# First attention: block-diagonal queries with 128-row maxima and score products, and the negated maxima sent by transfer into a contraction row

## The reference

```python
def _L0_xattn_ref(q, k, v, Wq, bq, Wk, bk, Wv, bv, Wo, bo):   # 16 heads of 8
    qh = (q @ Wq.T + bq).reshape(B, S, H, Hd).transpose(0, 2, 1, 3)
    kh = (k @ Wk.T + bk).reshape(B, S, H, Hd).transpose(0, 2, 1, 3)
    vh = (v @ Wv.T + bv).reshape(B, S, H, Hd).transpose(0, 2, 1, 3)
    scores = jnp.einsum('bhqd,bhkd->bhqk', qh, kh) / jnp.sqrt(jnp.float32(Hd))
    attn = jax.nn.softmax(scores, axis=-1)
    out = jnp.einsum('bhqk,bhkd->bhqd', attn, vh)
    out = out.transpose(0, 2, 1, 3).reshape(B, S, D)
    return out @ Wo.T + bo
x = x + _L0_xattn_ref(_layernorm(x, axis=-1), ctx_1024, ctx_1024, ...)
x = x + _L0_ffn_ref(_layernorm(x, axis=-1), ...)      # then the second layer
```

## Time and profile before

| | us |
|---|---|
| median of 3 runs (1695.71 to 1699.17) | 1699.14 |
| the profiled execution | 1695.49 |
| its span, first to last instruction | 1693.7 |
| TensorE matmul busy | 1401.0 (83%) |
| VectorE busy | 949.1 (56%) |
| ScalarE busy | 814.0 (48%) |
| GpSimd busy | 661.4 (39%) |

### The profile page before, as it was taken

One profiled execution on the slowest core, in us unless ns is written; L12 is line 12 of the kernel. 1 busy time (PEld: TensorE's weight loads), 2 busy tenths in 40 slices (PEclk: granted clock), 3 DMA queues, 4 the chain that ended last, 5 costly groups with the idle time before them and its releaser, 6 DMA issues. The chain is left out here.

```text
span 1693.7 us, 31779 instructions
## 1 busy us (share of the span) xinstructions
PE 1401.0 (83%) x11720; PEld 1123.0 (66%) x11720; DVE 949.1 (56%) x2066; ACT 814.0 (48%) x1335; POOL 661.4 (39%) x556
## 2 busy tenths in 40 slices
PE   0599999806599999999993798988988989836698
PEld 0477777606488888888882477777777777736486
DVE  0455544337656665666563666665666666527665
ACT  0255655521344444444442465655656556521354
POOL 1266656602155555555552123333232332412254
PEclk9999655555799999999996899998999899965799
DMA  4211111040000000000001000000000000010000
GB/s 114 75 39 39 46 63 45 2 149 1 1 1 1 1 1 1 0 0 0 0 0 62 1 2 1 2 1 3 2 1 3 2 1 2 2 32 1 1 25 25
DMA packets 27575, 31.59 MB, mean 19 GB/s; under 512 B 4721, under 2 KB 21682, under 8 KB 27314
## 3 DMA queue, kind: packets, MB, share of 16 engines
q1 hardware_dynamic: 27442, 29.75, 5.7%
HBM read 23.45 MB, written 6.29 MB: 18 GB/s over the span
## 5 line engine op out<-in xcount | busy, mean ns | idle before, releaser
L1347 POOL TENSOR_TENSOR w_lo_f<-weighted_f,w_hi_f 128x512 fp32r<-128x512 f32 x232 | 300.6, 1296 | 345.8 <-ACT w_hi_f L1289 345.8
L565 POOL TENSOR_TENSOR p_lo_l<-probs_l,p_hi_l 128x512 f16<-128x512 f32 x128 | 148.2, 1158 | 336.5 <-ACT p_hi_l L358 336.5
L1327 DVE TENSOR_TENSOR hidden_f<-psum,gate_act_f 128x512 f32<-128x512 f32 x232 | 160.5, 692 | 210.0 <-PE psum L1239 199.3
L1304 ACT ACTIVATE gate_act_f<-psum 128x512 f32<-128x512 f32 x232 | 138.7, 598 | 269.0 <-PE psum L1239 267.6
L916 POOL TENSOR_TENSOR p_lo_a<-probs_a,p_hi_a 128x1024 f16<-128x1024 f32 x64 | 135.9, 2127 | 112.9 <-ACT p_hi_a L808 112.9
L1333 DVE TENSOR_TENSOR weighted_f<-psum,hidden_f 128x512 f32<-128x512 f32 x232 | 160.5, 692 | 9.0
L1239 PE MATMUL psum<-x_lo_f,w_hi 128*128 (+1 forms) x384 | 153.8, 401 | 0.0
L1237 PE MATMUL psum<-x_hi_f,w_hi 128*128 (+1 forms) x384 | 152.0, 396 | 1.8 <-PEq L1135 1.8
L1238 PE MATMUL psum<-x_hi_f,w_lo 128*128 (+1 forms) x384 | 151.8, 395 | 0.0
L1289 ACT ACTIVATE w_hi_f<-weighted_f 128x512 fp32r<-128x512 f32 x232 | 144.9, 625 | 2.2 <-DVE weighted_f L1333 2.2
L356 ACT ACTIVATE probs_l<-psum,lift_l 128x512 f32<-128x512 f32 x128 | 88.0, 688 | 105.0 <-PE psum L232 105.0
(11 more groups left out here) (257 smaller groups left out, 3797.9 us busy)
## 6 DMA issues: line engine op xcount, KB each, us to landing
q_x_a<-spill SPq DMA_DIRECT2D x32, 128.0 KB, 2.6
k_x_a<-spill SPq DMA_DIRECT2D x32, 128.0 KB, 2.5
spill<-q_hl_a SPq DMA_DIRECT2D x8, 256.0 KB, 2.0
spill<-k_hl_a SPq DMA_DIRECT2D x8, 256.0 KB, 2.9
out<-x_all SPq DMA_DIRECT2D x8, 256.0 KB, 2.3
pick_raw<-c_pick SPq DMA_DIRECT2D x1, 1536.0 KB, 6.2
stage<-L_ffn_w SPq DMA_DIRECT2D x3, 256.0 KB, 3.0
stage<-L_xattn_Wq SPq DMA_DIRECT2D x1, 512.0 KB, 3.5
```

Source lines behind the costliest of these rows:

```text
L565: nc.gpsimd.tensor_tensor(p_lo[:, r, :], probs[:, r, :], p_hi[:, r, :], ALU.subtract).then_inc(s_exp_lo, 1)
L1304: nc.scalar.activation(gate_act[:, slot, :], GATE[slot][:, :], ACT.Silu).then_inc(s_silu, 1)
L1327: nc.vector.tensor_tensor(hidden[:, slot, :], UP[slot][:, :], gate_act[:, slot, :], ALU.mult).then_inc(s_hid, 1)
L1347: nc.gpsimd.tensor_tensor(w_lo[:, slot, :], weighted[:, (parity * nc_ + k) % 2, :], w_hi[:, slot, :].bitcast(F32), ALU.subtract).then_inc( ...
```

## The change

The four row groups are no longer used as separate small products. The queries go into a block-diagonal tensor `q_pad` with 128 rows: in slot (r, i) only the 32 rows of head 4r + i hold queries and the others are zero. The keys `k_x` keep their layout and are now used in one piece of 128 rows (four heads). So one product of 128 rows by 512 columns gives the scores of four heads; two of them replace the 16 in a step. The maxima are 8 products of 128 rows by 128 columns.

Row 3 of the 128 was a second copy of a product of two lower halves; it now holds 1 in the keys (written once, at the start) and in the queries the negated maximum, which is thus added by the contraction. The maxima are transposed as 16 rows by 128 queries, and SP sends them by one transfer a batch (`maxima_row`) from `negmax_t` to row 3 of `q_pad`. Until then the row must hold zero for the maxima products, which a transfer of `nothing` provides in each group. The scores wait for the row transfer instead of ScalarE's copy. Heads are now split over the two steps of a batch by r instead of i.

The query spread becomes 16 transfers of 8 partitions (one of 7) and one of the zero row; the key spread stays at 4, the last with 31 partitions. SP's loop now runs over steps. VectorE and GpSimd clear `q_pad`, VectorE sets `k_x` to 1. The selector and its block fall away.

```diff
-                for r in range(4):
-                    for i in (2 * j, 2 * j + 1):
...
-                        nc.tensor.matmul(o, k_x[rows, par, r, tok], q_x[rows, par, r, tok], start=True, stop=False)
...
-                        last_ = nc.tensor.matmul(o, sel[rows, r, :], negmax_t[rows, b % 2, :], start=False, stop=True)
+                for r in (2 * j, 2 * j + 1):
+                    last_ = nc.tensor.matmul(T_BANK[:, 2 * (s % 2) + r % 2, :], k_x[:, par, r, tok], q_pad[:, par, r, :, tok],
+                                             start=True, stop=True)
...
-                        last_ = nc.tensor.matmul(M_BANK[:, i % 2, r * P:(r + 1) * P], q_x[rows, par, r, tok],
-                                                 k_x[rows, par, r, tok], start=True, stop=True)
+                        last_ = nc.tensor.matmul(M_BANK[:, r % 2, i * P:(i + 1) * P], q_pad[:, par, r, i, tok],
+                                                 k_x[:, par, r, tok], start=True, stop=True)
...
+            def spill(g, m):
+                sp.wait_ge(s_lo, 5 * g + 3 + m)
+                if g:
+                    sp.wait_ge(s_spread, SPREADS * 16 * (g - 1) + (17 * 16 if m == 0 else SPREADS * 16))
+                sp.dma_start(dram[m, g % 2], (q_hl, k_hl)[m][:, :, :]).then_inc(s_spill, 16)
+
+            def spread(g, m):
+                sp.wait_ge(s_spill, 32 * g + 16 * m + 16)
+                if g >= 2:
+                    sp.wait_ge(s_sc, 8 * (g - 2) + 8)
+                halves = dram[m, g % 2].rearrange("(r p) l n -> l p r n", p=32)
+                if m == 0:
                     for t in range(4):
+                        for i in range(4):
+                            skip = int(t == 3 and i == 0)
+                            dst = q_pad[32 * i + t + 4 * skip:32 * i + 32:4, g % 2, :, i, :]
+                            sp.dma_start(dst, halves[t // 2, 8 * i + skip:8 * i + 8]).then_inc(s_spread, 16)
+                    rows = q_pad[3:4, g % 2, :, :, :].rearrange("o r i n -> o (r i) n")
+                    sp.dma_start(rows, nothing[:, :].unsqueeze(1).broadcast_to([1, H, 512])).then_inc(s_spread, 16)
+                else:
+                    for t in range(4):
+                        skip = int(t == 3)
+                        sp.dma_start(k_x[t + 4 * skip::4, g % 2, :, :], halves[t % 2, skip:32]).then_inc(s_spread, 16)
+
+            def maxima_row(b):
+                sp.wait_ge(s_nmt, b + 1)
+                tok = slice(b % GB * P, (b % GB + 1) * P)
+                dst = q_pad[3:4, b // GB % 2, :, :, tok].rearrange("o r i n -> o (r i) n")
+                sp.dma_start(dst, negmax_t[:, b % 2, :]).then_inc(s_row[b % 2], 16)
+
+            sp.wait_ge(s_clear, 2)
+            for s in range(FIRST, LAST):
+                if s % 2 == 0 and 0 <= s + LM0 - 2 < NP:
+                    maxima_row((s + LM0 - 2) // 2)
+                if (f := fill_of(s - 1)) and f[1] in (2, 3):
+                    spread(f[0], f[1] - 2)
+                if (f := fill_of(s)) and f[1] in (2, 3):
+                    spill(f[0], f[1] - 2)
...
-            nc.vector.memset(negmax[:, :, :], 0.0)
+            nc.vector.memset(nothing[:, :], 0.0)
+            nc.vector.memset(k_x[:, :, :, :], 1.0)
+            nc.vector.memset(q_pad[:, 0, :, :, :], 0.0).then_inc(s_clear, 1)
...
+            nc.gpsimd.memset(q_pad[:, 1, :, :, :], 0.0).then_inc(s_clear, 1)
             normal(0)
...
-            const["sel0"] = rounded("sel0", [P, 4, P], a["c_sel0"], scope)
```

More of the change, by code:

```diff
@@ L584 @@
 RING0 = 4
+SPREADS = 21
 def fill_of(s):
@@ L610, in sem @@
         return mem.enter_context(nc.semaphore(f"{name}_a0"))
-    ident, sel = const["ident"], const["sel0"]
+    ident = const["ident"]
     xhat = sb("xhat", [P, GB, D])
@@ L618, in attention0 @@
     q_hl, k_hl = sb("q_hl", [P, 2, 512], F16), sb("k_hl", [P, 2, 512], F16)
-    q_x, k_x = sb("q_x", [P, 2, 4, 512], F16), sb("k_x", [P, 2, 4, 512], F16)
+    q_pad, k_x = sb("q_pad", [P, 2, 4, 4, 512], F16), sb("k_x", [P, 2, 4, 512], F16)
+    nothing = sb("nothing", [1, 512], F16)
     v_hi, v_lo = sb("v_hi", [P, 2, GB, H, D0 + 1], F16), sb("v_lo", [P, 2, GB, H, D0 + 1], F16)
-    negmax, negmax_t = sb("negmax", [P, 2, P]), sb("negmax_t", [P, 2, P], F16)
+    negmax, negmax_t = sb("negmax", [P, 2, H]), sb("negmax_t", [H, 2, P], F16)
     probs = sb("probs", [P, 2, 1024])
@@ L630, in attention0 @@
     s_fill, s_hi, s_lo = sem("fill"), sem("hi"), sem("lo")
-    s_spill, s_spread = sem("spill"), sem("spread")
+    s_spill, s_spread, s_row = sem("spill"), sem("spread"), (sem("row_even"), sem("row_odd"))
+    s_clear = sem("clear")
     s_mm, s_max, s_nmt_mm, s_nmt = sem("max_mm"), sem("max"), sem("nmt_mm"), sem("nmt")
@@ L639, in _ @@
         def _(sp):
[L640 to L648, removed]
-                    for t in range(4):
-                        part = t // 2 if m == 0 else t % 2
-                        src = dram[m, g % 2].rearrange("(r p) l n -> l p r n", p=32)[part]
-                        sp.dma_start(wide[t::4, g % 2, :, :], src).then_inc(s_spread, 16)
+            def spill(g, m):
[3 more added lines that the diff above has]
+                sp.dma_start(dram[m, g % 2], (q_hl, k_hl)[m][:, :, :]).then_inc(s_spill, 16)
@@ L659, in scores @@
                 par = b // GB % 2
-                pe.wait_ge(s_nmt, b + 1)
+                pe.wait_ge(s_row[b % 2], 16 * (b // 2 + 1))
                 if s >= 2:
                     pe.wait_ge(s_exp_hi, s - 1)
-                for r in range(4):
-                    for i in (2 * j, 2 * j + 1):
-                        rows = slice(32 * i, 32 * i + 32)
-                        o = T_BANK[:, 2 * (s % 2) + i % 2, r * P:(r + 1) * P]
-                        nc.tensor.matmul(o, k_x[rows, par, r, tok], q_x[rows, par, r, tok], start=True, stop=False)
-                    for i in (2 * j, 2 * j + 1):
-                        rows = slice(32 * i, 32 * i + 32)
-                        o = T_BANK[:, 2 * (s % 2) + i % 2, r * P:(r + 1) * P]
-                        last_ = nc.tensor.matmul(o, sel[rows, r, :], negmax_t[rows, b % 2, :], start=False, stop=True)
+                for r in (2 * j, 2 * j + 1):
+                    last_ = nc.tensor.matmul(T_BANK[:, 2 * (s % 2) + r % 2, :], k_x[:, par, r, tok], q_pad[:, par, r, :, tok],
+                                             start=True, stop=True)
                 last_.then_inc(s_sc, 1)
@@ L678, in maxima @@
                 if s % 8 == 0:
-                    pe.wait_ge(s_spread, 128 * (s // 8) + 128)
+                    pe.wait_ge(s_spread, SPREADS * 16 * (s // 8 + 1))
                 if s >= 1:
                     pe.wait_ge(s_max, s)
-                for r in range(4):
-                    for i in (2 * j, 2 * j + 1):
-                        rows = slice(32 * i, 32 * i + 32)
-                        last_ = nc.tensor.matmul(M_BANK[:, i % 2, r * P:(r + 1) * P], q_x[rows, par, r, tok],
-                                                 k_x[rows, par, r, tok], start=True, stop=True)
+                for r in (2 * j, 2 * j + 1):
+                    for i in range(4):
+                        last_ = nc.tensor.matmul(M_BANK[:, r % 2, i * P:(i + 1) * P], q_pad[:, par, r, i, tok],
+                                                 k_x[:, par, r, tok], start=True, stop=True)
                 last_.then_inc(s_mm, 1)
@@ L702, in values @@
                     pe.wait_ge(s_x, b)
-                for r in range(4):
-                    for i in (2 * j, 2 * j + 1):
+                for r in (2 * j, 2 * j + 1):
+                    for i in range(4):
                         h = 4 * r + i
                         o = PV[:, h * (D0 + 1):(h + 1) * (D0 + 1)]
-                        q = slice((4 * (i % 2) + r) * P, (4 * (i % 2) + r + 1) * P)
+                        q = slice((4 * (r % 2) + i) * P, (4 * (r % 2) + i + 1) * P)
                         hi, lo = v_hi[:, par, b % GB, h, :], v_lo[:, par, b % GB, h, :]
@@ L779, in fill @@
                 elif kind < 4:
+                    m = kind - 2
                     if g:
-                        act.wait_ge(s_spill, 32 * (g - 1) + 16 * (kind - 1))
-                    m = kind - 2
+                        act.wait_ge(s_spill, 32 * (g - 1) + 16 * m + 16)
                     nc.scalar.activation((q_hl, k_hl)[m][:, 0, :], F_BANK, ACT.Identity,
@@ L812, in _ @@
                     if b >= 2:
-                        act.wait_ge(s_sc, 2 * b - 2)
-                    nc.scalar.activation(negmax_t[:, b % 2, :], F_BANK[:, 0:P], ACT.Copy, bias=lifted).then_inc(s_nmt, 1)
+                        act.wait_ge(s_row[b % 2], 16 * (b // 2))
+                    nc.scalar.activation(negmax_t[:, b % 2, :], F_BANK[0:H, 0:P], ACT.Copy, bias=lifted).then_inc(s_nmt, 1)
                 if fill_of(s):
@@ L854, in maxima @@
                     dve.wait_ge(s_nmt_mm, b - 1)
-                out = negmax[:, b % 2, 64 * j:64 * j + 64].rearrange("p (i n) -> p i n", n=32)[:, :, 0:4]
```

(9 more changed lines are left out.)

2 lines of the change are left out of this document (1 added, 1 removed).

## The result

The changed kernel takes 1775.49 us (median of 4 runs, 1774.7 to 1776.87) against 1697.43 us for the kernel before (4 runs, one more than above): ratio 1.0462, interval 1.0444 to 1.048. It is slower by 78 us. The profiled execution has a span of 1774.0 us against 1693.7.

The account below looks back on a forecast made before the run. TensorE's queue in program order was taken to set the pace. Start +6.8, prologue +13.4 and +1, six periods +50.1, last group +8.3 and rest 0 make +79.6 on 1695.5 us: 1775 us, range 1728 to 1808.

Parts of the forecast that it names:

- T0: Moment SP's queue spills a group's projected queries; six intervals forecast at 254.4 us instead of 204.3, +50.1.
- sel0: Selector block between 20.80 and 24.25 us, ahead of the first attention; its removal saves 3.45 us.
- Clearing: VectorE's fills of k_x and half of q_pad ahead of the layer statistics, on the path: plus 10.2 us.
- Query spread: On SP's queue, 17 query transfers at 0.63 us instead of four: 10.7 us instead of 2.5.
- Key spread: Last of four key transfers, 31 partitions (124 KB), goes on one DMA engine and lands in 8.1 us.
- The row transfer: One maxima transfer a batch, issue 0.4, landing about 2.2 us, hidden except while SP spreads; batch 6's waits behind the keys.
- The chain: Transfers from T0 to the scores of step 12: 25.2 us, making the period 42.4 us instead of 34.05.
- The clock: Whole stage read as at the lower level (1.2 GHz); ready backlog and some full clock give 2.5 us a period.
- Rival C: Clock rises and stays outside stalls, 1.56 times the work; period 37.8, +39, 1735 us; chance 0.14.
- A: Transfers go evenly, 31 rows land in 2.5 us; period 37.2, +38, 1733 us; chance 0.12.
- B: Small issues are cheap: 17 query issues at 0.48 us, 8.2 instead of 10.7; 1755 us; chance 0.15.
- D: Faster: upper clock, issues at 0.48 and even spreading; chain 17.5, period 30.1, -23, 1672 us; chance 0.11.

Follow-up runs that it names:

- The split: Changed kernel with the 31-row key transfer sent as 16 and 15 rows; 1734.1 us.
- the doubling: Changed kernel with two key transfers of 31 rows instead of one; 1813.2 us.
- e4_both: Changed kernel with the 31 rows as 16 and 15 and eight of 16 query transfers left out; 1692.51 us, ratio 0.9961 to the kernel before.
- e5_onchip: Changed kernel with queries landing compact by five transfers, VectorE placing them in q_pad, fills behind the first statistics; 1671.21 us, ratio 0.9837 to the kernel before.

## Why the prediction was right

The forecast was 1775 us, the median is 1775.5. That agreement is closer than its terms and in part luck: some were low and some high. By span, in us against the kernel before:

| term | predicted | measured | from |
|---|---|---|---|
| start, to T0 of group 0 | +6.8 | +5.4 | 54.20 - 48.77 |
| prologue, T0 to first maxima | +13.4 | +14.4 | 26.6 - 12.2 |
| first maxima to T0 of group 1 | +1 | +0.7 | 12.4 - 11.7 |
| six T0 intervals | +50.1 | +53.6 | 257.9 - 204.3 |
| last T0 to scores of step 52 | +8.3 | +10.1 | 27.0 - 16.9 |
| the rest of the stage | 0 | -3.0 | 45.0 - 48.0 |
| sum | +79.6 | +81.2 | 423.1 - 341.9; whole spans differ by 80.3 |

**sel0.** The first weight load is issued at 21.09 instead of 24.25 us, 3.2 of the 3.45 us predicted.

**Clearing.** 3.47 us for the keys as worked out, but 3.47 and not 7.0 for q_pad: the trace calls it 128x4096 uint32, the form that the prediction named beside its sum. There were 0.8 us gaps ahead of each fill that it had not counted. So the clearing cost 8.6 us (39.11 - 29.89, against 33.75 - 33.08 in the kernel before) and not 10.2. GpSimd's 6.92 us did lie beside VectorE's.

**Query spread.** 17 transfers were worked out at 0.63 us, 10.7 in all; they took 0.72 each and 0.6 for the last, 12.1 from 138.41 to 150.5. The row of the same form as the new transfers was the right one and still 0.09 short. Half the transfers left out took 5.7 us out of a group.

**Key spread.** 8.1 us for the 31 rows on one engine; measured 8.0 in the prologue (fourth issue at some 72.8, maxima at 80.79). The split, the doubling and the busy share of 0.07 show it. The Trainium skill's rule (DMA: Bandwidth & Descriptors, Why a DMA increments its semaphore by 16 and not by 1), the largest number of engines up to 16 that divides the partitions, so one for 31 and 15 for 15, is borne out for the 31 rows by the changed kernel and these two runs. The 15 rows agree with it: they landed in 2.7 us, like the others.

**The row transfer.** It waits as predicted behind the 31 rows, 7.8 us instead of 1.7, and so TensorE stops at the scores of step 8g+4, ahead of the maxima. All 7 waits of the kind are there (groups 1 to 7).

**The chain** is 163.32 - 136.41 = 26.9 us, not 25.2, and 1.4 of the 1.7 us between them are the query issues. From there to the next T0 it is 16.1 us, not 17.2. That quicker way goes with the clock, which was at the upper level for its last 7 us.

**The clock** is the step that was mis-sized. The prediction read the stage as at the lower level and granted 2.5 us a period for spells of the upper one. In fact it was at 1.00 for some 19 of the 43 us of a period (to 148.7 and again from 172.6 on, in the one from 136.41 to 179.44). So TensorE came to the scores of step 12 about 13 us after T0 instead of 17, and waited 14 us and not 6 to 9. The sign that I had named, a clock mostly at 0.50, held only just, for 24 of 43 us. Most of that gain went into the wait: while the chain of transfers decides, a quicker TensorE only waits longer. This is why the error hardly shows in the sum. Rival C had the clock rise outside the stalls, as it did, but credited 1.56 times the work to all of the way after the stall; it is slow for the first 9 us there. The reading that the page's 1.00 ahead of the first fall proves nothing is borne out: at 80.79 us the changed kernel too shows 1.00 at maxima that take 1.03 us, and at 147.91, also at 1.00, the same eight take 0.61.

**Rivals.** A and B are refuted by the landing and by the issue times. D named the right conditions: a short chain and the upper clock. With a chain of some 16.5 us made by hand (e4_both) the sign turned. With the block diagonal built on chip (e5_onchip) the result was 1671 us, where D had 1672. That the totals agree is chance. D had +6.8 at the start, -23.7 in the six periods and -13 in the rest; e5_onchip has -1.5 (T0 at 47.28), -18.6 (six of 30.95) and -3.7 (318.35 - 274.17 = 44.2 from the scores of step 52 to the end of the stage, against 47.9).

## What to carry to other kernels

Count what a change asks of the queue that issues the transfers, not only of the engines: here TensorE's new products were no loss in themselves, and 13 more issues of 0.72 us each and one 31-row transfer in each group went with a loss of 78 us, where a version with neither gained 28. A quicker engine ahead of such a chain only waits longer. When a transfer leaves out a row, look at the row count that remains: 31 rows went at the pace of one DMA engine here (8.0 us), and a small transfer issued behind them waited (7.8 us). As 16 and 15 rows they landed in 2.6 and 2.7. Where a layout must be scattered finely, bring it in compact by few transfers and scatter it with an engine that has idle time.

## What the runs showed of the hardware

- A DMA of 31 rows of 4 KB from SP's queue landed in 8.0 us, of 32 rows in 2.5; a 4 KB transfer issued behind it took up to 7.8 us instead of 1.7, behind two of them up to 11.7, behind 16 and 15 rows up to 3.5.
- The issue of a transfer of 8 partitions with a step of 4 kept SP for 0.655 us (median of 128), not less than that of 32 partitions (median of 32: 0.598 in the kernel before, 0.630 in the changed one).
- TensorE took 0.61 us for the eight maxima products of 128 rows at a granted clock of 1.00 (147.91 in the changed kernel) and 1.06 at 0.50 (164.36).
- GpSimd was slower beside VectorE's float16 copies: the four operations of 128 x 128 took 4.81 us in the one group where they overlap, against 3.13 or 3.14 in the seven others. Both are from the kernel with the block diagonal built on chip, by its timeline; GpSimd's operations beside the copies:

```profile
55.41 4.81 POOL L938 TENSOR_SCALAR xhat_a<-x_all,meanvar_a,rstd_a 128x128 f32<-128x128 f32 x4
```

One of the groups without copies beside them, and the copies themselves:

```profile
33.79 3.14 POOL L938 TENSOR_SCALAR xhat_a<-x_all,meanvar_a,rstd_a 128x128 f32<-128x128 f32 x4
...
55.23 2.78 DVE L898 COPY q_pad_a<-q_x_a 32x2048 f16<-32x2048 f16 x4 [1.33 <-DMA q_pad_a<-nothing_a]
```

That the one is the cause of the other is read from the overlap alone; no run was made for it.
